# A transformer block on one core: rows gathered by computed numbers, two expert blocks written out, gate scores turned around

## The chip, the cores and the metric

The kernel runs on one core of one Trainium2 chip. The metric is the device time in microseconds (us) of one launch; lower is better. Of the kernel before there are three runs: 826.24, 819.68 and 824.00 us, median 824.0.

Engines: TensorE (PE) multiplies, VectorE (DVE) and ScalarE (ACT) work elementwise, GpSimd (POOL) does small work and issues DMAs on a queue of its own, SyncE (SP) only issues DMAs, on another queue.

## The reference, cut to what matters

```python
x = x + tanh(g_xattn) * xattn(ctx, layernorm(x))     # 4 x 512 rows of 512
x = x + tanh(g_ffn)   * ffn(layernorm(x))

# xattn: sim = Q K^T per batch (512 x 512), its top 30% of each row kept,
#        A = sigmoid(sim) * mask;  (1-gamma) * input + gamma * (A + A^T) / 2
# ffn:
scores = xt @ gate_w.T                               # 2048 tokens, 8 experts
p, e = top_k(softmax(scores), 2);  p = p / p.sum()
y_e = (silu(xt @ w1[e].T) * (xt @ w3[e].T)) @ w2[e].T   # 512 -> 1024 -> 512, f32
out = sum over the two chosen experts of p_e * y_e
```

Counted with the reference on its own inputs, the experts get 504, 573, 522, 490, 526, 482, 490 and 509 tokens (expert 0: 240 of them from the first 1024 tokens).

## The kernel before

The work has two parts. Part 1 computes the new x for 4 batches of 4 tiles (128 rows each), finds for each token its two experts, and sorts the tokens by expert. Part 2 runs the expert layers in blocks of 128 tokens.

**Part 1, for batch b.** ACT takes the sigmoid of the similarities, DVE masks them (`mask_A`, L993), PE adds A and its transpose (`add_transposed`, L502 and L504), ACT copies the sum out of PSUM (`even_rows`, L685), DVE adds it to x (`x1`, L1001), and SP stores the new x into `out`. ACT sums the squares (`spreads`, L697), POOL makes scale and shift of the second layernorm (`row_scales`), ACT writes the normalised rows (`normal_rows`, L705). PE computes the gate scores (`even_scores`, L513) with the rows as stationary operand and the gates (8 columns) moving. DVE chooses the two best experts (`choose`, L1028 to L1078), PE ranks the tokens within their expert (`ranks`), and POOL scatters each row, with the expert weights and the token's number behind it, into the expert's region of `routed` in DRAM (`route`, L399): per batch 4 tiles times 2 choices, 32 scatters in all. After the last batch, DVE writes `table`: first and last block of each expert.

**Part 2.** One loop over the experts holds a loop over the blocks of an expert; every engine runs the same two loops and they meet through semaphores. In a block g:
- PE runs the first layer in two halves of 512 columns (gate into one bank, up into another, each product as three fp32r matmuls: high times high, low times high, high times low; L546 to L548), transposes h of half 0 (L568), the rows of block g+1 (`transpose_x`, L553) and h of half 1, and runs the second layer into bank 7. The second layer's first piece waits for `hT_set[0]`, the low part of h's transpose.
- ACT makes silu (L754), the high parts of h's transposes (L758) and of the next rows (L750).
- DVE makes the product (L1128), the low parts (L1132 for h, L1116 for x), and scales y by the expert weight (L1140).
- POOL adds y into `out` with an indirect DMA that accumulates (`add_blocks`, L434): it waits for `y_set`, computes `y_row` (L432), drains (L433) and issues.
- SP loads the rows of the next block from `routed` as soon as `xtile` is free (L324).

The weights of an expert are 6 MB in three pieces (`raw`). POOL issues the loads of expert e+1's pieces at the head of its loop over e (L442), when the low parts of expert e's pieces have been made. In the last block of an expert, ACT and DVE also split the arrived weights into high (`w_hi`, L670) and low parts (`w_lo`, L1010). For expert 0 this happens ahead of the loop (`first_low`, L1022, and `split_high`).

The number of blocks is 35: the tokens of each expert divided by 128, rounded up. Each engine's instructions run in the order in which the code writes them; there is no scheduler.

## Time and profile before

| | |
|---|---|
| median of three runs | 824.0 us (819.68 to 826.24) |
| the profiled execution, its own time | 824.68 us |
| its span | 823.0 us |
| PE busy | 732.0 us, 89% |
| DVE busy | 396.6 us, 48% |
| ACT busy | 286.8 us, 35% |
| POOL busy | 146.9 us, 18% |
| mean granted clock of TensorE | 0.918 |

The span is the profiled execution from its first to its last instruction. Busy times are of instructions that compute or issue a DMA; the sequencers' own steps (waits, drains, register loads) are not counted. Matmuls overlap, so a busy PE need not be at its peak.

### The profile page before, as it was taken

To read this page: it belongs to the slowest core of one execution; us is meant where nothing else is said; L and a number is where in the kernel's file an instruction comes from. 1 tells how busy PE (TensorE), PEld (TensorE's weight loads), DVE (VectorE), ACT (ScalarE), POOL (GpSimd) and SP (SyncE) were. 2 spreads that over 40 slices of the span, in tenths; PEclk is the share of its full clock that TensorE was granted. 3 is DMA by queue.
4 is the path that set the end of the run, shared out by engine and by line. 5 is a ranking of instruction groups with operands and counts; after the bars stand their busy time and mean duration, and the time that the engine had idled before them with its cause. 6 is when DMAs were issued, how large, how long until landed. Compare 5 with 4: busy or idle time off the path is not lost.

```text
span 823.0 us, 10904 instructions
## 1 busy us (share of the span) xinstructions
PE 732.0 (89%) x3370; PEld 589.9 (72%) x3371; DVE 396.6 (48%) x930; ACT 286.8 (35%) x475; POOL 146.9 (18%) x199
## 2 busy tenths in 40 slices
PE   7393079556999999999999999999999999999996
PEld 3193046545888888888888888888888888888885
DVE  3988966562247232832266229222652382265222
ACT  4754647621135211711154116112531261253111
POOL 1371002782111000011001011010011110101110
PEclk9655577568999999999999999999999999999999
DMA  8842032655622721182115511821155127211111
GB/s 302 324 161 102 12 142 106 239 200 191 231 38 62 288 41 43 26 324 46 39 26 180 203 26 26 331 38 39 35 197 177 28 40 315 51 36 29 26 30 22
DMA packets 23727, 98.18 MB, mean 119 GB/s; under 512 B 2784, under 2 KB 3040, under 8 KB 19872
## 3 DMA queue, kind: packets, MB, share of 16 engines
q0 software_dynamic: 10992, 66.21, 26.0%
q1 hardware_dynamic: 12576, 31.81, 11.3%
q8 instruction: 4, 0.07, 0.0%
q14 instruction: 11, 0.09, 0.0%
q10 hardware_dynamic: 144, 0.00, 0.0%
HBM read 73.72 MB, written 24.30 MB: 119 GB/s over the span
## 4 chain that ended last, share of the span: by engine, by line
issue 72%; DVE 9%; POOL 6%; PE 5%; POOLq 3%; ACT 2%; DVEq 1%; DMA 1%; SPq 0%; ACTq 0%
POOL out L434 4%; POOL routed L399 2%; DVE front L852 2%; PE bank L504 2%; POOLq L255 1%; POOLq L433 1%; PE bank L466 1%; PE bank L502 1%; DVE top L950 1%; DVE ln_stats L810 1%; DVE front L947 1%; DVE rows_own L827 1%; POOL raw L442 1%; ACT front L705 1%; PE bank L456 1%
## 5 line engine op out<-in xcount | busy, mean ns | idle before, releaser
L546 PE MATMUL bank<-w_hi,xT_hi 128*128 128x512 f32 x560 | 225.5, 403 | 3.3 <-DVE xT_lo L1116 3.3
L547 PE MATMUL bank<-w_hi,xT_lo 128*128 128x512 f32 x560 | 222.3, 397 | 0.0
L548 PE MATMUL bank<-w_lo,xT_hi 128*128 128x512 f32 x560 | 221.7, 396 | 0.0
L754 ACT ACTIVATE act_g<-bank 128x512 f32<-128x512 f32 x70 | 41.8, 596 | 332.1 <-PE bank L548 327.6
L546 PEld LDWEIGHTS bank<-w_hi,xT_hi 128*128 128x128 f32 x560 | 105.8, 189 | 27.5 <-issue 3.7
L548 PEld LDWEIGHTS bank<-w_lo,xT_hi 128*128 128x128 f32 x560 | 105.6, 188 | 25.8
L547 PEld LDWEIGHTS bank<-w_hi,xT_lo 128*128 128x128 f32 x560 | 105.8, 189 | 23.5
L546 PE MATMUL bank<-w_hi,hT_hi 128*128 128x512 f32 x280 | 115.9, 414 | 0.0
L1132 DVE TENSOR_TENSOR hT_lo<-bank,hT_hi 128x512 fp32r<-128x512 f32 x70 | 48.4, 692 | 138.7 <-ACT hT_hi L758 138.7
L1010 DVE TENSOR_TENSOR w_lo<-raw,w_hi 128x1024 fp32r<-128x1024 f32 x88 | 104.3, 1221 | 19.0 <-ACT w_hi L670 10.5
L670 ACT ACTIVATE w_hi<-raw 128x1024 fp32r<-128x1024 f32 x88 | 91.4, 1061 | 59.3 <-PE bank L548 50.4
L548 PE MATMUL bank<-w_lo,hT_hi 128*128 128x512 f32 x280 | 110.0, 393 | 0.0
L547 PE MATMUL bank<-w_hi,hT_lo 128*128 128x512 f32 x280 | 109.9, 392 | 0.0
L1128 DVE TENSOR_TENSOR h<-bank,act_g 128x512 f32<-128x512 f32 x70 | 48.4, 691 | 96.9 <-PE bank L548 92.4
L432 POOL TENSOR_TENSOR y_row<-token_out,no_shift 128x1 int32<-128x1 int32 x35 | 6.4, 183 | 458.1 <-DVE token_out L1141 458.1
L1140 DVE TENSOR_SCALAR y<-bank,meta_now 128x512 f32<-128x512 f32 x35 | 26.3, 750 | 104.9 <-PE bank L548 99.4
L434 POOL DMA_INDIRECT out<-y,y_row x35 | 58.1, 1661 | 86.2 <-issue 86.2
L548 PEld LDWEIGHTS bank<-w_lo,hT_hi 128*128 128x128 f32 x280 | 52.8, 189 | 11.5
L547 PEld LDWEIGHTS bank<-w_hi,hT_lo 128*128 128x128 f32 x280 | 53.1, 190 | 8.7
L546 PEld LDWEIGHTS bank<-w_hi,hT_hi 128*128 128x128 f32 x280 | 53.2, 190 | 8.5
L758 ACT ACTIVATE hT_hi<-bank 128x512 fp32r<-128x512 f32 x70 | 41.7, 595 | 20.6 <-PE bank L568 19.8
L568 PE MATMUL bank<-ident,h 128*128 128x128 f32 x280 | 42.4, 275 | 1.5 <-issue 1.5
(190 smaller groups left out, 668.8 us busy)
## 6 DMA issues: line engine op xcount, KB each, us to landing
raw<-weights POOLq DMA_DIRECT2D x21, 2048.0 KB, 15.7
xtile<-routed SPq DMA_DIRECT2D x36, 260.5 KB
raw<-weights SPq DMA_DIRECT2D x3, 2048.0 KB, 7.9
xb<-x SPq DMA_DIRECT2D x4, 1024.0 KB, 11.3
raw<-xT SPq DMA_DIRECT2D x4, 1024.0 KB, 9.0
w_hi<-weights POOLq DMA_DIRECT2D x2, 2048.0 KB, 10.3
out<-xb SPq DMA_DIRECT2D x4, 1024.0 KB, 4.2
routed<-pad SPq DMA_DIRECT2D x8, 260.5 KB, 2.3
```

Source lines behind the costliest of these rows:

```text
L434: nc.gpsimd.indirect_dma_start(out, bass.IndirectOffsetOnAxis(ap=y_row[:, 0:1], axis=0), y[:, :], None, bounds_check=TOKENS + P - 1, oob_i ...
L546: nc.tensor.matmul(out_ap, hi, hi_w, start=start, stop=False)
L547: nc.tensor.matmul(out_ap, lo, hi_w, start=False, stop=False)
L548: return nc.tensor.matmul(out_ap, hi, lo_w, start=False, stop=stop)
L568: last = nc.tensor.transpose(bank[H_BANK[s]][:, c * P:(c + 1) * P], h[:, s, c * P:(c + 1) * P], ident[:, :])
L670: nc.scalar.activation(w_hi[q][:, j, :], raw[:, q, j * OPW:(j + 1) * OPW], ACT.Copy).then_inc(hi_set[q], 1)
L754: nc.scalar.activation(act_g[:, s, :], bank[GATE[s]][:, :], ACT.Silu).then_inc(silu_set[s], 1)
L758: nc.scalar.activation(hT_hi[:, s, :], bank[H_BANK[s]][:, :], ACT.Copy).then_inc(hhi_set[s], 1)
L1010: V.tensor_tensor(w_lo[q][:, j, :], raw[:, q, j * OPW:(j + 1) * OPW], w_hi[q][:, j, :].bitcast(F32), ALU.subtract).then_inc(lo_set[q], 1)
L1128: V.tensor_tensor(h[:, s, :], bank[UP[s]][:, :], act_g[:, s, :], ALU.mult).then_inc(h_set[s], 1)
L1132: V.tensor_tensor(hT_lo[:, s, :], bank[H_BANK[s]][:, :], hT_hi[:, s, :].bitcast(F32), ALU.subtract).then_inc(hT_set[s], 1)
L1140: V.tensor_scalar(y[:, :], bank[Y_BANK][:, :], meta_now[:, bass.ds(e, 1)], None, ALU.mult).then_inc(y_out, 1)
```

## The change

1. **No rows are scattered.** x1 is stored twice, into `out` and into `found` (one row per token in its own order, 128 rows of padding ahead). Behind each row stand its expert weights, its number, and scale and shift of its layernorm (`meta`, stored for two batches at a time; `store_meta`). `normal_rows` and `route` are gone.
2. **Blocks gather their rows.** POOL's `gather` is an indirect DMA from `found` into `xtile` by 128 row numbers in `rows_now`. ACT normalises the gathered rows in place (`normal_x`), one pass of 128x512 per block. SP has no part in the loop any more.
3. **Row numbers are computed.** For each of the 32 picks DVE writes a one-hot matrix of the slot (128x128), and DVE or POOL two of the column (128x136 each, times the partition's or the tile's number); PE multiplies them into `rows_ps` (`all_blocks`, 32 matmuls of 272 columns), DVE sorts the columns by block with table entries read one by one (`order_blocks`). For the two first blocks of expert 0, which take their tokens from the first half and from what follows, a smaller version is used (`early_slots`, `early_blocks`, `early_rows`).
4. **Two blocks are written out** ahead of the loops on all engines, with the choice for the second half of the tokens, the table and the row numbers between their instructions. The choice runs for two batches at a time.
5. **Scores.** `even_scores` has the gates as stationary operand (8 columns) and the rows moving (512 columns); ACT copies the 8x512 result, PE turns it back with four transposes per batch (`turn_scores`).

```diff
@@ sync @@
-            sp.wait_ge(early_set, 1)
-            early_full = sp.value_load(early_blocks[0:1, 0:1], min_val=0, max_val=TOKENS // P)
...
-                        sp.dma_start(xtile[:, :], routed[bass.ds(e * REGION + j * P, P), :]).then_inc(xtile_in, 16)
...
+                sp.dma_start(found_x[b], xb[:, b, :, :]).then_inc(x1_found[b], 16)
                 sp.dma_start(out_tiles[b], xb[:, b, :, :]).then_inc(x1_stored[b], 16)
@@ gpsimd @@
-            row_scales(0)
-            row_scales(1)
-            route(0, range(TB))
...
+            def gather(at):
+                nc.gpsimd.indirect_dma_start(
+                    xtile[:, :], None, found, bass.IndirectOffsetOnAxis(ap=at, axis=0),
+                    bounds_check=P + TOKENS - 1, oob_is_err=True,
+                ).then_inc(xtile_in, 16)
...
+            def add_y(g, and_next_x=True):
...
+                pool.wait_ge(y_set, g + 1)
+                nc.gpsimd.tensor_tensor(y_row[:, :], token_out[:, :], no_shift[:, :], ALU.add)
+                pool.drain()
+                if and_next_x:
+                    gather(rows_now[:, 0:1])
+                nc.gpsimd.indirect_dma_start(
+                    out, bass.IndirectOffsetOnAxis(ap=y_row[:, 0:1], axis=0), y[:, :], None,
...
+            pool.wait_ge(xtile_free, 1)
+            gather(rows_now[:, 0:1])
+            columns_of_first(range(PICKS // 4, PICKS))
+            add_y(0, and_next_x=False)
+            next_weights(0)
+            pool.wait_ge(xtile_free, 2)
+            gather(rows_now[:, 0:1])
+            add_y(1)
+            pool.wait_ge(table_set, 1)
+            add_blocks(0)
+            with pool.Fori(1, E - 1) as e:
+                next_weights(e)
                 add_blocks(e)
@@ tensor @@
+                for c in range(DC):
+                    last = nc.tensor.matmul(turned_ps[b], gate_c[:, c, :], even[b][:, c, :], start=(c == 0), stop=(c == DC - 1))
...
+            for g in range(WRITTEN):
...
+                if g == 1:
+                    all_blocks(0)
+                    all_blocks(1)
+                pe.wait_ge(hT_set[0], nth)
...
+                pe.wait_ge(hT_set[1], nth)
+                for k in range(1, OPS):
...
+                    if k == OPS - 1:
+                        transpose_x(nth + 1)
+                    second_layer([2 * k, 2 * k + 1]).then_inc(piece_done[2], 1)
@@ scalar @@
+            def normal_x(n):
...
+                act.wait_ge(xtile_in, n * 16)
+                nc.scalar.activation(xtile[:, 0:D], xtile[:, 0:D], ACT.Identity, bias=xtile[:, SHIFT:SHIFT + 1],
+                                     scale=xtile[:, SCALE:SCALE + 1]).then_inc(xn_set, 1)
...
                         silu(0, nth)
+                        normal_x(nth + 1)
                         silu(1, nth)
@@ vector @@
+            slots(1)
+            x_low(2, rows=False)
+            columns_of_second()
+            scale_y(0, 0, OPS)
+            take_meta()
...
+            tabulate()
+            product(0, 2, 2 * OPS)
+            h_low(0, 2)
+            product(1, 2, 2 * OPS)
+            order_blocks()
+            next_rows(2).then_inc(xtile_free, 1)
+            h_low(1, 2)
+            x_low(3)
```

How the order moves is shown at three places. The first is POOL's queue at the head of part 2, in the kernel before: weights (L442), then per block y_row and the adding scatter (drains and waits don't show as rows).

```order
L399 DMA routed<-rows_own,place_i 17408x521 x8
L439 UNCONDITIONAL_BRANCH
L439 ISA
L442 ISA
L442 DMA raw<-weights 128x4096
L442 ISA
L442 DMA raw<-weights 128x4096
L442 ISA
L442 DMA raw<-weights 128x4096
L255 REGISTER_ALU
```

And the same place of the change: scatter of block 0, weights of expert 1 (L471), the gather for block 2 (L426), then block 1 and a block of the loop.

```order
L459 TENSOR_TENSOR y_row<-token_out,no_shift 128x1
L463 DMA out<-y,y_row 2176x512
L471 DMA raw<-weights 128x4096 x3
L426 DMA xtile<-found,rows_now 128x523
L459 TENSOR_TENSOR y_row<-token_out,no_shift 128x1
L426 DMA xtile<-found,rows_now 128x523
L463 DMA out<-y,y_row 2176x512
L286 TENSOR_LOAD table
```

The loads of x's rows, which stood on SP's queue, now stand on POOL's, between y_row and the scatter, and behind the weights where these come first.

The second place is a block without new weights on ACT, before:

```order
L753 REGISTER_ALU
L754 ACTIVATE act_g<-bank 128x512 x2
L758 ACTIVATE hT_hi<-bank 128x512
L749 REGISTER_ALU
L750 ACTIVATE xT_hi<-bank 128x512
L758 ACTIVATE hT_hi<-bank 128x512
```

and now (L884 is silu, L834 is `normal_x`, L888 the high part of h, L839 that of x):

```order
L884 ACTIVATE act_g<-bank 128x512
L833 ISA
L834 ACTIVATE xtile<-xtile 128x512
L884 ACTIVATE act_g<-bank 128x512
L888 ACTIVATE hT_hi<-bank 128x512
L839 ACTIVATE xT_hi<-bank 128x512
L888 ACTIVATE hT_hi<-bank 128x512
```

`normal_x`, which waits for the gather, stands ahead of silu of half 1 and of both high parts of h.

The third is DVE in block 1 of the change, where nothing stood before but product and low parts: the end of `order_blocks` (one of its eight table loads is shown), the row numbers of block 2, then `h_low(1)` (L1353), for which PE's second layer waits.

```order
L286 TENSOR_LOAD table
L286 ISA x2
L1324 ISA
L1324 TENSOR_SCALAR rows_at<-scratch,part_no 128x17
L1328 TENSOR_SCALAR rows_now<-zero,rows_at 128x1
L1353 TENSOR_TENSOR hT_lo<-bank,hT_hi 128x512
L1333 COPY meta_next<-xtile 128x8
```

DVE's low part of h now stands behind the whole of `order_blocks`.

## Rows read from the trace of the kernel before

**Rows 1.** The page's slices: granted clock of TensorE, in tenths, 40 equal slices.

```profile
PEclk9655577568999999999999999999999999999999
```

**Rows 2.** Timeline, PE: start, us, engine, line, op, out<-in, count, [idle before <-releaser].

```profile
174.64 0.79 PE L546 MATMUL bank<-w_hi,xT_hi 128*128 128x512 f32 x1 [3.34 <-DVE xT_lo L1116]
...
194.87 1.11 PE L553 MATMUL bank<-ident,xtile 128*128 128x128 f32 x4 [4.76 <-DMA xtile<-routed]
...
196.21 0.63 PE L547 MATMUL bank<-w_hi,hT_lo 128*128 128x512 f32 x1
...
203.30 0.40 PE L546 MATMUL bank<-w_hi,xT_hi 128*128 128x512 f32 x1
...
797.30 0.40 PE L546 MATMUL bank<-w_hi,xT_hi 128*128 128x512 f32 x1
```

**Rows 3.** Timeline, POOL, around the weights of expert 2.

```profile
260.49 1.97 POOL L434 DMA_INDIRECT out<-y,y_row  x1 [0.92 <-issue]
261.91 2.26 POOL L442 DMA_DIRECT2D raw<-weights  x3
276.59 0.18 POOL L432 TENSOR_TENSOR y_row<-token_out,no_shift 128x1 int32<-128x1 int32 x1 [12.42 <-DVE token_out L1141]
284.54 1.67 POOL L434 DMA_INDIRECT out<-y,y_row  x1 [7.76 <-issue]
```

**Rows 4.** Lines L433 and L442: count, durations in ns min/median/max; time to landing.

```profile
L433 POOLq DRAIN  x35: 357/360/12912, 204.5 to 816.5; - x35
...
DMA to landing us min/median/max: 7.8/15.7/20.7
```

**Rows 5.** Timeline, POOL: two of the 32 scatters of rows.

```profile
170.36 1.97 POOL L399 DMA_INDIRECT routed<-front,place_i  x1 [0.30 <-issue]
...
176.18 0.98 POOL L399 DMA_INDIRECT routed<-front,place_i  x1 [0.30 <-issue]
```

**Rows 6.** The chain that ended last (start, us, what), and landing times of L434.

```profile
188.78 2.81 DMA routed<-rows_own,place_i
...
DMA to landing us min/median/max: 4.6/4.9/5.3
```

**Rows 7.** Timeline of DVE, groups by form (busy, mean ns | idle), and line L255.

```profile
125.97 2.74 DVE L993 SCALAR_TENSOR_TENSOR front<-front,thr 128x512 f32<-128x512 f32 x4 [0.72 <-ACT front L676]
...
159.79 0.37 DVE L1031 MAX8 best<-score 128x8 f32<-128x8 f32 x4
...
164.96 0.17 DVE L1078 CAST place_i<-place_f 128x8 int32<-128x8 f32 x1
...
165.72 8.04 DVE L1022 TENSOR_TENSOR w_lo<-raw,w_hi 128x1024 fp32r<-128x1024 f32 x7
...
L852 DVE TENSOR_SCALAR_CACHE_REDUCE front<-front,probe 128x512 bf16<-128x512 f32 x24 | 16.6, 742 | 0.7
...
L705 ACT ACTIVATE rows_own<-xb,ln_o,ln_r 128x512 f32<-128x512 f32 x8 | 5.8, 801 | 0.0
...
L255 DVEq TENSOR_LOAD <-table x24: 300/303/321, 184.6 to 748.2; - x24
```

**Rows 8.** Timeline of the block that starts at 275.3.

```profile
280.41 0.60 ACT L754 ACTIVATE act_g<-bank 128x512 f32<-128x512 f32 x1 [9.10 <-PE bank L548]
...
286.42 0.69 DVE L1132 TENSOR_TENSOR hT_lo<-bank,hT_hi 128x512 fp32r<-128x512 f32 x1 [4.59 <-ACT hT_hi L758]
...
286.94 0.60 PE L553 MATMUL bank<-ident,xtile 128*128 128x128 f32 x4
287.29 0.48 PE L546 MATMUL bank<-w_hi,hT_hi 128*128 128x512 f32 x1
```

**Rows 9.** Timeline, POOL, the last scatter.

```profile
817.70 1.55 POOL L434 DMA_INDIRECT out<-y,y_row  x1 [0.92 <-issue]
```

**Rows 10.** The chain that ended last: PE in part 1.

```profile
119.53 0.86 PE bank L504 x2
...
121.69 4.33 PE bank L513 x32
```

More of the change, by code:

```diff
@@ L492, in _, with add_transposed @@
             nc.tensor.matmul(settled_ps, ones_f[:, :], settled[:, :], start=True, stop=True).then_inc(settled_mm, 1)
[L494 removed]
+            def add_transposed(b, tiles):
                 At = A[b % 2]
                 pe.wait_ge(A_set, b + 1)
[L498 removed]
+                for i in tiles:
                     if b > 0:
@@ new lines, in order_blocks @@
+            def order_blocks():
+                dve.wait_ge(rows_mm, 2)
+                V.tensor_copy(region_rows_at[:, :], rows_ps[:, 1, :])
+                dve.drain()
+                V.scalar_tensor_tensor(region_rows_at[:, :], region_rows_at[:, :], float(P), rows_ps[:, 0, :], ALU.mult, ALU.add)
+                dve.drain()
+                dve.wait_ge(table_set, 1)
+                for e in range(E):
+                    at = 0 if e == 0 else entry(dve, 0, e, 1, MOST_BLOCKS - 1)
+                    V.tensor_scalar(rows_at[:, bass.ds(at, PER)], region_rows_at[:, e * PER:(e + 1) * PER], part_no[:, :], None, ALU.max)
+                    dve.drain()
```

674 lines of the change are left out of this document (425 added, 249 removed).

## The prediction

> **What bounds it now.** I read the slices first. In the last thirty of forty TensorE (PE) has its full clock, 2.4 GHz; in the ten before that the granted clock lies between that and 1.2 GHz, since PE is starved there [rows 1]. Then the timeline of PE: the first block of the expert layers starts at 174.64, the second at 203.30, the thirty-fifth at 797.30 [rows 2]. So 33 blocks take 594.0 us, 18.0 each; only the first is long, 28.7: PE waits 4.76 us for the second block's rows, and behind that wait a matmul lasts 0.63 us, as at 1.2 GHz, not 0.40 [rows 2]. The kernel is a front, then a loop at the pace of PE. A change can gain only by starting block 2 (counted from 0; at 221.3 now) earlier, and it loses whatever it puts into the loop, once per block or once per expert.
>
> The third view is POOL's queue. A 2 MB piece of weights is issued there three times per expert. Each time, the next block's scatter waits: y_row is computed at 276.59, but the scatter comes at 284.54, with 7.76 us of idle before it [rows 3], where the last one of the kernel has 0.92 [rows 9]. Seven of the 35 scatters are like this, one per set of weights. The drain between y_row and the scatter is what lasts: median 0.36 us, up to 12.9; the three pieces land one after the other, 7.8, 15.7 and 20.7 us after issue [rows 4]. 284.54 is 22.6 us behind 261.91 [rows 3], so POOL goes on when the 6 MB have landed. Now that costs nothing: nobody needs the scatter within a block, and the next rows come over SP's queue.
>
> **The change, part by part.** *The loop.* x's rows now come by a gather on POOL, behind that drain. Everywhere else it is early enough: issued 2.4 us into a block (as the scatter at 817.70, behind a block that ends at 815.3 [rows 9]), wanted behind silu(0), at 5.7 (280.41 and 0.60 [rows 8]). But in the second block of experts 1 to 6 it meets the weights. I lay it into the block that starts at 275.3. The scatter stood at 284.54; in the last block of the expert before, a gather goes ahead of scatter and weights, and one indirect DMA takes 1.3 us of POOL (0.98 and 0.3 idle) [rows 5], so the weights and all behind them are 1.3 later: gather at 285.8. The trace has no gather. Nearest rows: a scatter's rows land in 2.81 us, a scatter-add in 4.9 [rows 6]. A gather adds nothing up, so I take 2.8: 288.6. Then ACT, in its order, has normal_x (0.80, as L705 [rows 7]), silu (0.60), h_high (0.6), and DVE h_low (0.69): 289.4, 290.0, 290.6, 291.3, and with 0.1 us from engine to engine PE can start its second layer at 291.6. It starts at 287.29 now, right behind the transposes of x at 286.94 [rows 8]. **The loss is 4.3 us**, six times: 26 us. Bounds: 2.2 if the gather lands in 2.0 and the weights aren't moved; 6.4 if it lands like a scatter-add. normal_x itself is hidden elsewhere, since ACT has nothing else between silu(0) and silu(1); in a block with new weights it delays one copy of w_hi by 0.75 us, and the copies behind it wait for PE anyway. If that cover were gone, it would cost 0.75 in each of seven blocks. No block is added: the reference's own choice on its inputs gives expert 0 504 tokens, 240 of them in the first half, so four blocks as before, and 35 in all.
>
> The Trainium skill has a rule on POOL's DMAs beside wide work of DVE (SBUF — State Buffer, "SBUF: two separate sides"): descriptors are written through a port that DVE can lock, and a DMA of 620 ns then takes 3100. The trace agrees in kind, not in size: the two rows of rival 3 below show one us. At the page's factor of five the sum would be some 30 us higher, by the rows' one us it is the 6 of that rival.
>
> *The front.* Choosing and placing now happen twice, for eight tiles at a time; block 0 starts after the first half. DVE's order decides. Its third masking starts at 125.97 and takes 2.74 [rows 7]; ACT now squares batch 0's rows (four passes of 128x512) later, so I let it end at 127.3. Behind it on DVE, up to the y of block 0: twelve subtracts of 1.15 (8.04 for seven [rows 7]), 13.8; two choices (one of four tiles runs from its MAX8 at 159.79 to 164.96 [rows 7], 5.4 with its ends; four more tiles and ten more small steps make it 9.2), 18.4; fifteen passes of 128x512 (x1, x_low, product, h_low, scale_y) at 0.69 [rows 8], 10.4; small steps, 2.1: 44.7. DVE waits too: PE has its first eight tiles at 121.7, where the gate scores start now, and then needs two times four 0.86 for the new scores, two more tiles and eight short transposes [rows 10], to 132.4, when DVE has been ready since 129.7; with 2.0 for the transposes of the second x, 4.7. New are 88 instructions of 128x128 or 128x136 that write one-hot rows: 128x8 takes 0.09, 128x512 0.74 [rows 7]. A line through both gives 0.24; a bf16 source may be quicker, down to 0.09. I take 0.16: 14.1 (8 to 21). The gate scores themselves took 4.33 us a batch [rows 10] and take four times 0.86 and four transposes, about 4: under 1 us of PE a batch, beside DVE. So y_set comes at 127.3 + 44.7 + 4.7 + 14.1 = 190.8, and behind it y_row, drain, scatter, then the weights of expert 1: 2.7 later, **193.5**.
>
> Block 0 itself starts near 160, 14 us earlier, and that gain isn't kept: block 1 needs the rows of block 2, whose gather stands behind these weights, with or without a drain, since pieces on this queue land in order [rows 4]. 193.5 + 20 (19 to 22, between a piece's 20.7 to landing and the 22.6 to the next indirect DMA, less its start) + 2 for the gather is 215.5; normal_x 0.8; PE has idled by then, so transposes at the slow level, 1.1 as at 194.87, and six matmuls at half the loop's pace (18.0 us for 72 and some transposes), 2.6 [rows 2]: block 2 starts at **220.0** instead of 221.3, a gain of 1.3. Also in block 1, DVE's eight loads of table entries (0.30 each plus arithmetic [rows 7]) stand ahead of h_low(1): some 7 us that PE would wait, covered by the longer wait for the gather. Without that wait they would be next.
>
> *The end.* The last gather stands ahead of the last scatter: the scatter stands at 817.70 now [rows 9]; 1.3 us more.
>
> **Sum.** 823.0 − 1.3 + 6 x 4.3 + 1.3 = 848.8 of span. The profiled execution took 824.68 for its 823.0, and that is 0.7 above the median of three: 848.8 + 1.7 − 0.7 = 850.
>
> **Rivals.**
> 1. *The clock falls too.* In the held block PE is idle for 2.7 us and again for 1.5. After 4.76 us of idle a matmul took 0.63 instead of 0.40 [rows 2], some ten times, 2 us lost. If that happens in the six blocks: 850 + 12 = 862. Against it: both idle pieces are much shorter than that one, with work between.
> 2. *The hold is nearly hidden.* The gather lands in 2 us and the weights aren't later: 2.2 per expert, 850 − 13 = 837.
> 3. *DVE delays POOL's DMAs.* Indirect DMAs took 1.97 us while DVE ran wide subtracts and 0.97 otherwise [rows 5]. DVE runs such subtracts when an expert's last gather, scatter and weights are issued. One us more for each of the gather and weights: six times 1, 856. This is the mechanism of the Trainium skill's rule above (SBUF — State Buffer).
> 4. *The gather isn't held* (the other side): the drain passes, or the gather's rows overtake the weights. From 0 us of hold on, only the front decides: block 1 then waits for the eight loads, block 2 starts near 217, and the end is 823.0 − 4 + 1.3 + 1 = 821, no change; if the one-hot instructions cost 0.09, 6 us less, 815, faster. Against it: all seven drains behind weights were long, none was short.
>
> **Chances.** Forecast (846 to 854) 0.55; the clock 0.14; nearly hidden 0.10; DVE's delay 0.05; not held 0.12; 0.04 for a front that is later than any of these. The range takes the forecast, the clock and the nearly hidden case: front 7 us better with 2.2 per expert gives 830; front 8 us worse with 6.4 gives 870, which need not meet: 829 to 868. A median can tell about 1% (8 us) from no change. Over 1% slower is above 832: all but rival 4 and a little of 2, 0.82. Within 1%: 0.13. Faster by over 1%: rival 4 with cheap one-hot work, 0.05.
>
> **What would show it.** PE should wait for normal_x or the gather in one block of each of experts 1 to 6, about 4 us, and in no other; the drain should last about 7 us there; silu(1) should follow normal_x late in these blocks. The first matmul of block 0 should stand near 160 and that of block 2 near 220. I am wrong if the loop has no waits (rival 4), if the waits are there at other places too, or if block 2 starts before 212.

## The result and the profile after

| | before | after |
|---|---|---|
| median | 824.1 us (819.68 to 826.24, 4 runs) | 867.9 us (863.37 to 869.25, 4 runs) |
| the profiled execution, its own time | 824.68 us | 868.96 us |
| its span | 823.0 us | 867.4 us |
| PE busy | 732.0 us | 749.6 us |
| POOL busy | 146.9 us | 186.2 us |
| mean granted clock of TensorE | 0.918 | 0.913 |

The changed kernel is slower: ratio 1.055, 95% interval 1.051 to 1.059. The forecast was 850 with a range of 829 to 868; the measured median lies on its upper edge, 18 us above the forecast.

The granted clock by slices, from the page of the kernel after. It answers to [rows 1]: where the kernel before has nines without a break, there are now six eights. Four of them are slices with a held block of the loop; the first is the end of block 1 and the last is the end of the kernel. The two held blocks with the shortest slow stretches don't show at this width.

```profile
PEclk9655599796899899998999999989999999899998
```

The front, from the timeline of PE (start, us, engine, line, op, out<-in, count, [idle before <-releaser]); it answers to [rows 2].

```profile
156.42 0.79 PE L608 MATMUL bank<-w_hi,xT_hi 128*128 128x512 f32 x1 [5.14 <-DVE xT_lo L1337]
...
181.81 0.50 PE L608 MATMUL bank<-w_hi,xT_hi 128*128 128x512 f32 x1 [0.15 <-DVE xT_lo L1337]
...
201.15 1.12 PE L630 MATMUL bank<-ident,h 128*128 128x128 f32 x4 [9.30 <-DVE h L1349]
...
218.74 0.79 PE L608 MATMUL bank<-w_hi,hT_hi 128*128 128x512 f32 x1 [7.24 <-DVE hT_lo L1353]
...
226.40 0.49 PE L608 MATMUL bank<-w_hi,xT_hi 128*128 128x512 f32 x1 [0.37 <-DVE xT_lo L1337]
```

Block 0 starts at 156.42 and block 1 at 181.81, 18 and 21 us earlier than before. In block 1 PE stands twice, for h (9.30) and for the low part of h (7.24), and block 2 starts at 226.40, which is 5.1 later than before. The timelines of DVE and POOL say what stands ahead of these waits:

```profile
176.84 3.05 DVE L1222 TENSOR_SCALAR xb<-from_one,slot 128x128 bf16<-128x128 bf16 x16
...
196.25 0.06 DVE L1235 MEMSET small<- 128x1 f32 x1 [7.21 <-POOL scratch L420]
...
217.56 0.23 DVE L1324 TENSOR_SCALAR rows_at<-scratch,part_no 128x17 f32 x1 [0.77 <-issue]
```
```profile
189.33 0.81 POOL L419 TENSOR_SCALAR scratch<-columns,column,part_no 128x136 bf16<-128x136 bf16 x1
...
199.64 2.29 POOL L471 DMA_DIRECT2D raw<-weights  x3
218.90 1.13 POOL L426 DMA_INDIRECT xtile<-found,rows_now  x1 [16.96 <-DVE rows_now L1328]
```

POOL writes its 24 one-hot columns of the second half from 173.5 to 195.8: 0.81 to 1.06 us each, but one of 2.46 beside DVE's wide subtracts, 0.93 on average. DVE, whose 16 one-hot slots take 3.05, is done with its own columns at 189 and stands 7.21 us for them, ahead of block 0's y. So the weights are issued at 199.64. In block 1 the eight parts of the table come one per 1.01 us up to 217.56. Expert 0's needs no table entry, so there are seven loads and not eight; between two parts DVE is idle for 0.77 to 0.81 us, of which 0.30 is the load and the rest is register work. Only then comes block 2's gather.

The loop, at the same place as [rows 3] and [rows 8]: the block behind the weights of expert 2. First POOL and ACT, then PE, then stretches of PE (us, busy and count of PE, PEld, DVE, ACT, POOL, granted clock, DMA share, GB/s).

```profile
268.51 2.23 POOL L471 DMA_DIRECT2D raw<-weights  x3
281.72 0.18 POOL L459 TENSOR_TENSOR y_row<-token_out,no_shift 128x1 int32<-128x1 int32 x1 [10.98 <-DVE token_out L1359]
290.83 1.11 POOL L426 DMA_INDIRECT xtile<-found,rows_now  x1 [8.93 <-issue]
...
294.32 0.81 ACT L834 ACTIVATE xtile<-xtile 128x512 f32<-128x512 f32 x1 [8.19 <-DMA xtile<-found,rows_now]
```
```profile
291.80 0.39 PE L610 MATMUL bank<-w_lo,xT_hi 128*128 128x512 f32 x1
295.19 0.66 PE L615 MATMUL bank<-ident,xtile 128*128 128x128 f32 x4 [3.00 <-ACT xtile L834]
296.88 0.80 PE L608 MATMUL bank<-w_hi,hT_hi 128*128 128x512 f32 x1 [1.04 <-DVE hT_lo L1353]
297.48 0.63 PE L609 MATMUL bank<-w_hi,hT_lo 128*128 128x512 f32 x1
...
302.59 0.40 PE L610 MATMUL bank<-w_lo,hT_hi 128*128 128x512 f32 x1
```
```profile
281.00:291.00 10.00, 10.00 (x47) 8.11 (x46) 1.57 (x5) 0.60 (x1) 0.36 (x2) 1.00 0.67 285
...
297.00:302.00 5.00, 5.00 (x14) 4.04 (x15) 1.97 (x6) 0.60 (x1) 0.00 (x0) 0.50 0.00 0
303.00:308.00 5.00, 5.00 (x23) 4.06 (x23) 1.07 (x4) 0.00 (x0) 0.18 (x1) 1.00 0.00 0
```

The gather is issued 9.1 us behind y_row, where 1.2 us is usual, and its rows land 3.5 us behind that. PE idles 3.00 and 1.04 us, and after that it runs at a granted clock of 0.50 (the level of 1.2 GHz) up to 302.6: 14 matmuls in 5 us instead of 23. This block takes 25.1 us where an ordinary one takes 18.0. It is the longest of the six: they are 5.4 to 7.2 us too long. The waits of PE from 230 us on (waited for: us in total, times, longest) show that this happens in six blocks and nowhere else; below them the drain ahead of the gather (count, ns min/median/max), and the gather's time to landing.

```profile
PE bank L615 <- ACT xtile L834: 16.8, 6, 3.1
PE bank L608 <- DVE hT_lo L1353: 4.8, 6, 1.0
```
```profile
L460 POOLq DRAIN  x35: 448/451/8379, 197.2 to 859.3; - x35
```
```profile
DMA to landing us min/median/max: 3.4/3.5/4.3
```

Added up: block 2 starts 5.1 us later; from there to the end of the last block (858.0) it takes 631.6 us instead of 594.0, so 37.6 more for six held blocks, 6.3 each; from there to the end of the span 9.4 instead of 7.7, 1.7 more. 823.0 + 5.1 + 37.6 + 1.7 = 867.4, the span after.

### The profile page after: what moved, and what is told of

Read it like the earlier page. It is cut to its first block, busy times and chain, and to the rows that moved or that the text cites. A ratio compares the mean times of both kernels' runs of the same rounds, so it can differ in the third digit from the quotient of the medians.

```text
span 867.4 us, 10544 instructions
## 1 busy us (share of the span) xinstructions
PE 749.6 (86%) x3344; PEld 587.1 (68%) x3345; DVE 416.7 (48%) x1046; ACT 304.7 (35%) x497; POOL 186.2 (21%) x246
## 4 chain that ended last, share of the span: by engine, by line
issue 66%; DVE 11%; POOL 10%; PE 6%; POOLq 3%; DVEq 2%; DMA 1%; SPq 0%; ACT 0%
POOL out L463 5%; POOL xtile L426 2%; DVE front L988 2%; POOL scratch L420 1%; POOL scratch L419 1%; PE bank L554 1%; PE bank L516 1%; POOLq L460 1%; POOLq L286 1%; DVE top L1090 1%; PE bank L563 1%; DVE ln_stats L946 1%; DVE front L1087 1%; DVE scratch L963 1%; PE bank L552 1%
## 5 line engine op out<-in xcount | busy, mean ns | idle before, releaser
L884 ACT ACTIVATE act_g<-bank 128x512 f32<-128x512 f32 x70 | 41.6, 594 | 279.3 <-PE bank L610 279.3
L608 PE MATMUL bank<-w_hi,hT_hi 128*128 128x512 f32 x280 | 122.0, 436 | 15.0 <-DVE hT_lo L1353 15.0
L1353 DVE TENSOR_TENSOR hT_lo<-bank,hT_hi 128x512 fp32r<-128x512 f32 x70 | 48.3, 691 | 159.8 <-ACT hT_hi L888 159.8
L609 PE MATMUL bank<-w_hi,hT_lo 128*128 128x512 f32 x280 | 114.1, 407 | 0.0
L610 PE MATMUL bank<-w_lo,hT_hi 128*128 128x512 f32 x280 | 114.0, 407 | 0.0
L1150 DVE TENSOR_TENSOR w_lo<-raw,w_hi 128x1024 fp32r<-128x1024 f32 x88 | 104.1, 1225 | 14.8 <-ACT w_hi L797 13.7
L608 PEld LDWEIGHTS bank<-w_hi,hT_hi 128*128 128x128 f32 x280 | 55.8, 199 | 27.6 <-DVE hT_lo L1353 18.3
L426 POOL DMA_INDIRECT xtile<-found,rows_now x37 | 43.3, 1170 | 122.0 <-issue 81.0
L610 PEld LDWEIGHTS bank<-w_lo,hT_hi 128*128 128x128 f32 x280 | 55.5, 198 | 12.8
L609 PEld LDWEIGHTS bank<-w_hi,hT_lo 128*128 128x128 f32 x280 | 56.1, 200 | 9.2
L888 ACT ACTIVATE hT_hi<-bank 128x512 fp32r<-128x512 f32 x70 | 41.7, 595 | 50.6 <-PE bank L630 50.6
L463 POOL DMA_INDIRECT out<-y,y_row x35 | 55.8, 1593 | 11.5 <-issue 11.5
## 6 DMA issues: line engine op xcount, KB each, us to landing
raw<-weights POOLq DMA_DIRECT2D x21, 2048.0 KB, 15.7
```

What stands on the lines that cost most here:

```text
L426: nc.gpsimd.indirect_dma_start(xtile[:, :], None, found, bass.IndirectOffsetOnAxis(ap=at, axis=0), bounds_check=P + TOKENS - 1, oob_is_err ...
L463: nc.gpsimd.indirect_dma_start(out, bass.IndirectOffsetOnAxis(ap=y_row[:, 0:1], axis=0), y[:, :], None, bounds_check=TOKENS + P - 1, oob_i ...
L608: nc.tensor.matmul(out_ap, hi, hi_w, start=start, stop=False)
L609: nc.tensor.matmul(out_ap, lo, hi_w, start=False, stop=False)
L610: return nc.tensor.matmul(out_ap, hi, lo_w, start=False, stop=stop)
L884: nc.scalar.activation(act_g[:, s, :], bank[GATE[s]][:, :], ACT.Silu).then_inc(silu_set[s], 1)
```

## The experiments

Each kernel is the changed one with the edit shown, if nothing else is said. Times are medians; the kernel before took 820.7 to 824.6 beside them.

**1. Weights on the other queue.** The change's cost in the loop should vanish if POOL's queue is what holds the gather, and stay if it is the traffic.

```diff
@@ sync, at its end @@
+            with sp.Fori(0, E - 1) as e:
+                for q in range(GROUPS):
+                    sp.wait_ge(lo_set[q], OPS * e + OPS)
+                    sp.dma_start(raw[:, q, :], w_groups[bass.ds(e + 1, 1), q, :, :].squeeze(0)).then_inc(raw_in[q], 16)
@@ gpsimd @@
-            next_weights(0)
...
-                next_weights(e)
```

> The changed kernel with the loads of experts 1 to 7's weights issued by SP, each under the same wait for the low parts, and none of them on POOL. Theory (the gather is held on POOL because POOL's drain and queue stand behind the weights): no block of experts 1 to 6 waits for its rows, all 33 blocks from block 2 take 18.0 us, the span falls by the 37.6 us of the six held blocks, to about 830 us; block 2 still starts near 226, since its gather was issued at 218.9 by the row numbers' time. Rival (the gather is late because 6 MB of weights fill the DMA engines, whoever issues them): the waits stay, 850 to 868 us.

Measured: 830.4 us, ratio 1.009 (1.006 to 1.012). The waits of PE from 230 us on, all of them, and POOL in the block that was held:

```profile
PE bank L610 <- DVE hT_lo L1355: 1.0, 1, 1.0
```
```profile
279.45 0.18 POOL L463 TENSOR_TENSOR y_row<-token_out,no_shift 128x1 int32<-128x1 int32 x1 [12.70 <-DVE token_out L1361]
280.65 1.07 POOL L430 DMA_INDIRECT xtile<-found,rows_now  x1 [1.02 <-issue]
```

The gather comes 1.2 us behind y_row, as in any block. Block 2 starts at 224.17, 2.2 us earlier than in the changed kernel, which I had not expected. So of the 43.8 us that the change costs, 37.5 hang on the queue on which the weights are issued, those 2.2 included. One wait of 1.0 is left; what it is comes with experiment 7.

But the edit moves more than the queue. SP issues the three pieces between 251.4 and 265.2, where POOL issues them at 268.5, when its own loop gets there. The last piece lands at 274.0, and between 275 and 280 us no DMA moves anything (the last two numbers of the row, DMA share and GB/s):

```profile
275.00:280.00 5.00, 5.00 (x23) 4.12 (x22) 1.06 (x4) 0.00 (x0) 0.18 (x1) 1.00 0.00 0
```

So this run alone doesn't rule out its rival, that the traffic holds the gather whoever issues it. Experiments 7 to 9 do.

**2. The transposes of x later.** The loop has them ahead of the second piece of the second layer; here they stand ahead of its last piece, as in the two written-out blocks, with `normal_x`, `x_high` and `x_low` moved behind h.

```diff
@@ tensor, in the loop @@
-                    transpose_x(nth + 1)
                     pe.wait_ge(hT_set[0], nth)
...
+                    transpose_x(nth + 1)
                     pe.wait_ge(lo_set[2], split[3])
                     second_layer([6, 7])
```

> The changed kernel with the transposes of the next block's rows put ahead of the last two pieces of the second layer in the loop, as in the two written-out blocks, and normal_x and the high and low parts of x behind those of h; the weights stay on POOL. Theory (only the distance from the held gather's landing, 13.9 us into the block, to its use counts): use at about 16.4, no waits of PE, 830 us, perhaps 1 to 3 more where DVE's low part of x ends after 18.0 in blocks with new weights. Rival (PE is slowed by something else beside the weights, not by the wait for rows): 860 us or more.

Measured: 869.6, ratio 1.058 (1.053 to 1.062): none of what was expected. The late rows no longer hold anything, but every block is now 19.0 us long. From 230 us on the only wait of PE is the first row below; the second is its place in an ordinary block.

```profile
PE bank L608 <- DVE xT_lo L1338: 19.0, 32, 1.5
```
```profile
319.75 0.49 PE L608 MATMUL bank<-w_hi,xT_hi 128*128 128x512 f32 x1 [0.35 <-DVE xT_lo L1338]
```

Only six matmuls, 1.4 us, stand between the transposes and the first matmul of the next block, and two copies have to run in between. That gives 0.35 us of idle and a gap in the matmuls around it, 1.0 us in each block, and 1.45 of idle and 2.1 us in all in the blocks in which DVE and ACT also split weights. 33 blocks of one us and more pay for what six blocks save. My expectation had 1 to 3 us in all for this, and not what the early place is good for. The time alone would have spoken for the rival, 860 or more; the waits show that it is this cost and not the rival's.

**3. normal_x behind silu(1) and h_high(0)**, in blocks without new weights.

```diff
@@ scalar, blocks without new weights @@
                         silu(0, nth)
-                        normal_x(nth + 1)
                         silu(1, nth)
                         h_high(0, nth)
+                        normal_x(nth + 1)
                         x_high(nth + 1)
```

> The changed kernel with normal_x behind silu of half 1 and behind the high part of h of half 0, on ACT in blocks without new weights. PE still waits 3.0 us for the transposes of x in the six held blocks, but no longer 1.0 for the low part of h. If the loss of 6.3 a block is 4.0 of waits and 2.2 of slower matmuls, and the clock falls all the same: 6 times 1.0 less, 862 us. If the clock fell because of the second wait: 6 times 3.2 less, 849 us. Rival (the order on ACT doesn't matter): 868 us.

Measured: 855.9, ratio 1.041 (1.037 to 1.046). The held block, in PE's timeline and in stretches:

```profile
294.56 1.12 PE L615 MATMUL bank<-ident,xtile 128*128 128x128 f32 x4 [2.86 <-ACT xtile L834]
```
```profile
295.00:297.00 2.00, 2.00 (x9) 1.60 (x8) 0.66 (x4) 0.60 (x1) 0.00 (x0) 0.50 0.43 77
298.00:303.00 5.00, 5.00 (x24) 4.12 (x23) 0.82 (x2) 0.45 (x1) 0.00 (x0) 1.00 0.00 0
```

PE still waits 2.86 us for the rows, but not a second time, since silu(1) and h's high part are ready; and the clock is back at 1.00 by 298, where in the changed kernel it stays at 0.50 up to 302.6. This is again the longest of the six. In the four last of them PE waits 1.8 to 2.4 us and the clock doesn't fall at all, as in the third:

```profile
483.00:487.00 4.00, 3.06 (x18) 2.62 (x19) 1.55 (x5) 2.01 (x3) 0.00 (x0) 1.00 0.51 66
```

So the order in ACT's queue decides over the second wait and over most of the slow stretches: 12 us in all, although an ordinary block has become 0.27 longer (18.24). The time lies between my 862 and 849. Both had taken the first wait as unchanged, but it is shorter too (13.7 us in six blocks instead of 16.8), so how much of the clock's part is due to which wait is not separated.

**4. Only the row numbers that are needed first.** Expert 0's part of the table is put in place ahead of block 2's gather, the other seven behind `h_low(1)`.

```diff
@@ vector @@
-                for e in range(E):
-                    at = 0 if e == 0 else entry(dve, 0, e, 1, MOST_BLOCKS - 1)
-                    V.tensor_scalar(rows_at[:, bass.ds(at, PER)], region_rows_at[:, e * PER:(e + 1) * PER], part_no[:, :], None, ALU.max)
+                V.tensor_scalar(rows_at[:, 0:PER], region_rows_at[:, 0:PER], part_no[:, :], None, ALU.max)
...
             h_low(1, 2)
+            order_rest()
```

> The changed kernel with only expert 0's row numbers computed ahead of block 2's gather and of h_low of block 1, and the seven experts with a table load each behind it. PE's wait of 7.2 us for the low part of h in block 1 should go. Theory of the prediction (this gather stands behind the weights issued at 199.6, landed at 220.3): block 2 starts at most 1 to 2 us earlier, 866 us. Rival (the gather isn't held there, having no drain ahead of it, and only the row numbers were late): it lands near 215, block 2 starts 8 to 9 us earlier, 859 us.

Measured: 864.4, ratio 1.052 (1.047 to 1.057). POOL and ACT:

```profile
198.95 2.29 POOL L471 DMA_DIRECT2D raw<-weights  x3
210.35 1.12 POOL L426 DMA_INDIRECT xtile<-found,rows_now  x1 [9.12 <-DVE rows_now L1332]
...
220.36 0.81 ACT L834 ACTIVATE xtile<-xtile 128x512 f32<-128x512 f32 x1 [10.38 <-DMA xtile<-found,rows_now]
```

The gather is issued 8.5 us earlier and its rows are there only 10 us later, 21.4 us behind the weights' issue. There is no drain ahead of this gather. So the weights hold a gather in two ways: a drain lets it be issued only when they have landed, and one that is issued without a drain has its rows only 0.6 us behind the last piece (landed at 219.7). Block 2 starts at 224.70. The Trainium skill says in "DMA: Bandwidth & Descriptors" (Two DMAs through the same engine are not ordered) that within one queue of one DMA engine descriptors start in order. These rows agree with it.

**5. POOL's columns shared out.** Six of POOL's picks of the second half (12 of 24 instructions) go to DVE.

```diff
@@ gpsimd @@
-            columns_of_first(range(PICKS // 4, PICKS))
+            columns_of_first(range(PICKS // 4, PICKS - 6))
@@ vector, at the head of columns_of_second @@
+                for m in range(PICKS - 6, PICKS):
+                    i, k = m // 2, m % 2
+                    V.tensor_scalar(in_column[0][:, m, 0, :], columns[:, :], column[:, 0, i, k:k + 1], part_no[:, :], ALU.is_equal, ALU.mult)
+                    V.tensor_scalar(in_column[0][:, m, 1, :], columns[:, :], column[:, 0, i, k:k + 1], tile_no[:, i:i + 1],
+                                    ALU.is_equal, ALU.mult)
```

> The change, with 6 of POOL's second-batch picks (12 of its 24 column instructions of 128x136) given to DVE. Theory (the front is late because POOL's column instructions take 0.81 to 0.98 us each, which the prediction didn't price, and DVE stands 7.2 us for them ahead of block 0's y): POOL ends some 11 us earlier, DVE has 12 x 0.2 = 2.4 us more to do, so y_set(0), T of the weights and all behind them come 4.8 us earlier; the wait for the gather of block 2 moves by the same, block 2 starts near 221.6 instead of 226.4, and the time is 867.9 - 4.8 = 863. Rival (DVE itself is what is late, by one-hot instructions of 0.19 to 0.23 instead of 0.16, and the wait for POOL only covers it): DVE's work gets 2.4 us longer, no gain or a loss of up to 2.4: 868 to 870.

Measured: 863.4, ratio 1.049 (1.044 to 1.053). POOL and PE:

```profile
193.78 0.19 POOL L459 TENSOR_TENSOR y_row<-token_out,no_shift 128x1 int32<-128x1 int32 x1 [7.01 <-DVE token_out L1364]
```
```profile
197.71 1.11 PE L630 MATMUL bank<-ident,h 128*128 128x128 f32 x4 [4.86 <-DVE h L1354]
...
222.62 0.50 PE L608 MATMUL bank<-w_hi,xT_hi 128*128 128x512 f32 x1 [0.36 <-DVE xT_lo L1342]
```

As the theory had it. POOL now waits for DVE, not DVE for POOL, and block 2 starts 3.8 us earlier. An instruction of this shape takes 0.81 us or more on POOL; on DVE the next one starts 0.23 us later.

**6. The old scores.** The rows stationary, the gates moving, 16 matmuls of 8 columns per batch, no turning back.

```diff
@@ tensor, even_scores @@
-                for c in range(DC):
-                    last = nc.tensor.matmul(turned_ps[b], gate_c[:, c, :], even[b][:, c, :], start=(c == 0), stop=(c == DC - 1))
+                for i in range(TB):
+                    for c in range(DC):
+                        last = nc.tensor.matmul(scores_ps[b // 2][:, b % 2 * TB + i, :], even[b][:, c, i * P:(i + 1) * P], gate_c[:, c, :],
+                                                start=(c == 0), stop=(c == DC - 1))
```

> The change, with the gate scores as in the kernel before: rows as stationary operand, 16 matmuls of 8 columns for a batch, written where they are wanted, no copy and no turning back. Prediction's claim: the turned form saves under 1 us of PE a batch beside DVE, so this kernel is within 1 us of the changed one: 867 to 869. Rival 1 (the turned form shortens the path in the front): block 0 starts 3 to 6 us later, but what that costs is at most what reaches block 2's gather: up to 871. Rival 2 (the turned form with its copies and transposes lengthens the path to the choice): earlier by 1 to 2 us: 866.

Measured: 870.8 (863.5 to 874.1), ratio 1.060 (1.056 to 1.065). Block 0 starts at 161.97, 5.6 us later than in the changed kernel, y_row of block 0 comes 4.7 later and block 2 at 229.63, 3.2 later. That is rival 1: the turned scores do shorten the path to block 0, and a part of that reaches block 2. Whether it reaches the end can't be told: the time itself moved less than its runs are apart.

**7. Weights on SP, and fewer row numbers first**; and the same with POOL's columns shared out. The seven other parts of the table stand behind block 1's y here.

> The change with two edits: the weights of experts 1 to 7 are issued by SP instead of POOL, and of the eight parts of the table of row numbers only expert 0's is put in place ahead of block 2's gather and h_low(1); the other seven come behind block 1's y (right as long as expert 0 has at least four blocks, as it has here). Theory: row_first gained only some 2 us since its gather, issued 8.5 us earlier, then stood behind the weights in POOL's queue; with these on another queue the gather is issued near 209.7, lands 3.5 us later, and PE's transposes of the rows come at 214.2 instead of 221.2; block 2 starts near 216.3 instead of 224.2 (the kernel with the weights on SP alone): 830.4 - 7.9 = 822.5. Rival (the weights' own traffic holds the gather, whatever the queue, or the seven table loads now delay block 2): 828 to 831.

> The three edits together: weights on SP, only expert 0's row numbers ahead of block 2, and 12 of POOL's column instructions on DVE. Theory: the three costs stand one after the other on the path to block 2, so they add: 830.4 - 7.9 - 4.8 = 817.7, block 2 near 211.5, and the kernel is faster than the one before by 0.8%. Rival (behind POOL's columns DVE's own order is next, so the split gives at most 2 us here): 820 to 822, no difference from before that can be told.

Measured: 827.7 (825.2 to 834.8), ratio 1.007 (1.004 to 1.009), and 828.7 (824.7 to 832.9), ratio 1.005 (1.003 to 1.008). Both missed. Block 2 does start early, at 217.65 and 217.42. What took it back, from the second kernel (POOL, ACT, PE):

```profile
172.97 1.17 POOL L430 DMA_INDIRECT xtile<-found,rows_now  x1 [13.31 <-DMA found<-meta]
```
```profile
181.69 0.81 ACT L836 ACTIVATE xtile<-xtile 128x512 f32<-128x512 f32 x1 [6.37 <-DMA xtile<-found,rows_now]
```
```profile
230.33 1.12 PE L632 MATMUL bank<-ident,h 128*128 128x128 f32 x4 [2.86 <-DVE h L1360]
```

Three things. First, SP issues expert 1's weights at 168.7, and block 1's gather, issued into this traffic at 172.97, lands after 8.7 us instead of 3.5. DVE stands 4.55 us for these rows (for their high part, up to 184.41), so that the shared-out columns gain nothing: y_row comes at 196.25, not at 193.8. Second, the seven table parts make the product of block 2 late by 2.86 us, and the slow clock behind it takes more: from y_row to y_row this block takes 23.1 us, 18.7 with the weights on SP alone. Third, in single blocks of the loop a gather is issued into the traffic of the weights and lands late: in the second kernel the weights of one expert are issued from 430.0 to 444.2, the gather at 442.1, and ACT has its rows at 450.5, 8.4 us later. Each such block is 1.2 to 3.9 us longer. Three of them are the same blocks in both profiles, but by other amounts, and the second kernel has one more; this may be what spreads the runs. The one wait left in experiment 1 is of this kind (its gather took 7.7 us). So a gather beside the weights on another queue is not free of them. But it isn't held until they have landed, as on POOL's: the gather of 172.97 has its rows at 181.7, ahead of the second piece (183.5), and that of 442.1 ahead of the third (454.1). All three were mended in the next step.

**8. The gather as early as it can go.** Every block from block 1 on issues the next gather as soon as the tile is free, ahead of y_row, drain and scatter. The wait is carried by an addition of zeros into an added buffer `spare`, four bytes a partition.

```diff
@@ gpsimd, add_y @@
+                if and_next_x:
+                    pool.wait_ge(xtile_free, g + 2)
+                    nc.gpsimd.tensor_tensor(spare[:, :], no_shift[:, :], no_shift[:, :], ALU.add)
+                    gather(rows_now[:, 0:1])
                 pool.wait_ge(y_set, g + 1)
                 nc.gpsimd.tensor_tensor(y_row[:, :], token_out[:, :], no_shift[:, :], ALU.add)
                 pool.drain()
-                if and_next_x:
-                    gather(rows_now[:, 0:1])
```

> The change, weights still on POOL, but in every block from block 1 on POOL issues the next gather as soon as the tile is free (some 14 us into the block before) and ahead of y_row, its drain and the scatter. Theory (what holds the rows is the 6 MB ahead of them in POOL's queue, and a gather without a drain ahead waits there too): in the block behind the weights the gather is issued near 14 us into the block before, but its rows land only when the weights have, 20 to 23 us behind their issue, some 9.5 to 11 us into the held block, which is 3 to 4 us earlier than in the changed kernel, since neither drain nor issue nor its own 3.5 us come behind them: PE's waits shrink from 4.0 to 0 to 1 us and the clock stays up: 867.9 minus 6 x 5.3 to 6.3, 830 to 836, and the landing time of these six gathers is over 10 us. Rival 1 (only the drain held it): landing 3.5 us in all of them, no waits, 829. Rival 2 (the rows begin to move only when all of the weights have landed and need 3.5 us from there): waits of 2 to 3 us stay, 850 to 858.

> The same early gather, with the weights of experts 1 to 7 issued by SP. Theory (on another queue the weights cost the gather only contention: some gathers issued under their traffic landed after up to 9.1 us instead of 3.5, and that made one or two blocks late): with 14 us of lead no block waits for its rows, and the last gather no longer stands ahead of the last scatter: 830.4 - 1.3 (end) - 1.6 (the one late block) = 827.5. Rival (POOL's early issue with its wait in front delays y's scatter or the next rows): 830 or more.

> All repairs together: early gather; weights on SP, those of expert 1 only once block 1's rows have landed; 12 of POOL's column instructions on DVE; only expert 0's row numbers ahead of block 2, each other expert's at the head of the loop over the expert before it (one us each, right as long as each expert has two blocks or more and expert 0 four). Theory: y of block 0 near 193.8 as with the columns split, block 2 some 20.9 us behind it as with only one table part ahead (196.8 to 217.7 there), at 214.7; then 33 blocks of 18.0 and 8.1 to the end: 816.8 of span, 818. Rival (in three_parts the seven table parts behind block 1 cost a wait of 2.9 us and a slow stretch; if the single ones at each expert's head cost DVE the same, product of half 0 is late once per expert): 818 + 7 x 1 = 825, no gain on the kernel before.

Measured: 819.3 (ratio 0.997, 0.995 to 0.999), 820.5 (0.998, 0.995 to 1.000) and 807.3 (0.983, 0.980 to 0.986; one of its six runs took 1497 us, for which I have no explanation, the others 806.9 to 808.2). The last ratio's interval reaches across 0.98, so whether it is 2% faster is unclear; that it is faster is clear. None of the three has a wait of PE left from 230 us on. With the weights on SP, all 33 gathers of the loop land after 3.3 to 3.6 us, nine of them issued while weights are moving:

```profile
DMA to landing us min/median/max: 3.3/3.5/3.6
```

That rules out the rival of experiment 1, in which the traffic alone holds them. But each kernel is 7 to 11 us faster than its theory, and the blocks take 17.73 us, not 17.97. The next experiment takes this apart; its kernel without the added buffer is the one to read for the gather alone.

**9. The four bytes.** `spare` behind `y_row` moves all later buffers by 32 bytes a partition, since the program rounds their addresses up. Two kernels have it without any new instruction, two have the early gather or all repairs without it.

```diff
         y_row = sb("y_row", [P, 1], I32)
+        spare = sb("spare", [P, 1], I32)
```

> The changed kernel with an unused buffer of four bytes a partition behind y_row, as the kernels with the early gather have it; no instruction differs. Theory A (where the buffers lie sets the pace of the first layer's matmuls, 0.227 us apart instead of 0.233): blocks take 17.73 us where they aren't held, 33 x 0.24 = 8 us less, 860. Theory B (the gather's time in the block sets it): 868, matmuls 0.233 apart.

> The early gather with weights on POOL, its waiting instruction writing into an unused column of an existing buffer, so that no buffer moves. Theory A (where the buffers lie): blocks of 17.97 again, 819.3 + 8 = 827. Theory B (when the gather runs): 819.

> The kernel before with the same unused buffer behind y_row. Theory A: if its blocks of 18.00 us have the same cause, 33 x 0.24 = 8 us less at most, 816 (its y_row stands behind other small buffers, so it may also be unmoved: 824). Theory B: 820 to 824, no change.

> All repairs together as in best, without the added buffer. Theory A: 807.3 + 8 = 815. Theory B: 807.

Measured: the changed kernel with the buffer 863.0 (ratio 1.046, 1.041 to 1.051), blocks of 17.73 us; the early gather without it 829.0 (1.005, 1.004 to 1.007), blocks of 17.96; the kernel before with it 824.0 (1.001, 0.998 to 1.004), blocks of 18.03; all repairs without it 816.5 (0.992, 0.988 to 0.995). Theory A holds in the family of the changed kernel: some 8 us of the gain in experiment 8 have nothing to do with the gather. The spans of the profiled executions are 825.6 against 817.9 for the early gather and 813.8 against 805.3 for all repairs. The medians differ by 9.7 and 9.2, but they come from two chips, on which the kernel before took 820.7 and 824.6. A group of first-layer matmuls by shape (busy, mean ns) between 230 and 860 us, of the changed kernel and with the buffer:

```profile
L609 PE MATMUL bank<-w_hi,xT_lo 128*128 128x512 f32 x523 | 206.2, 394 | 0.0
```
```profile
L610 PE MATMUL bank<-w_hi,xT_lo 128*128 128x512 f32 x521 | 202.8, 389 | 0.0
```

And this is the early gather without it, POOL and ACT at the place that was held, and the time to landing:

```profile
265.51 2.23 POOL L473 DMA_DIRECT2D raw<-weights  x3
274.15 0.19 POOL L460 TENSOR_TENSOR rows_at<-no_shift 128x1 int32<-128x1 int32 x1 [6.41 <-DVE rows_now L1330]
274.90 1.10 POOL L426 DMA_INDIRECT xtile<-found,rows_now  x1 [0.56 <-issue]
```
```profile
287.39 0.82 ACT L836 ACTIVATE xtile<-xtile 128x512 f32<-128x512 f32 x1 [2.90 <-DMA xtile<-found,rows_now]
```
```profile
DMA to landing us min/median/max: 3.4/3.5/12.5
```

The gather is issued 9.4 us behind the weights, lands 21.9 us behind them, after 12.5 us instead of 3.5, and PE's transposes of these rows come 2.2 us after they are normalised. So the rows wait in the queue as they did in experiment 4, and nothing waits for them. It is so in all six places: the rows land after 9.9 to 12.5 us, 0.6 to 0.7 behind the last piece of the weights. That rules out that only the drain held them. The medians give 867.9 - 829.0 = 38.9. The profiled executions are 41.7 us apart: 39.2 from block 1's y_row to the last one, 1.4 behind it, where the last gather is out of the last scatter's way, and 1.1 in the front.

## Why the prediction was right or wrong, point by point

- **What is held, and where: right.** One block each of experts 1 to 6, no other; PE waits for `normal_x`; the cause is the weights ahead in POOL's queue. w_on_sp removes it, early_no_pad removes it in another way. Rival 4 is out: on POOL's queue no gather passed the weights, with a drain or without.
- **The size of the hold: wrong; this is the step that failed most.** The term was 6 x 4.3 = 26; it measured 37.6, 11.8 more. The delay itself was worked out well: I had the gather 10.5 us into the block, the rows 13.3 and the second layer 16.3; in the block shown (it starts at 280.43) they stand at 10.4, 13.9 and 16.45. The gather lands after 3.5 us, not 2.8, and the steps behind it are shorter by 0.4. Of the 6.3 us, 3.6 are idle time of PE (21.6 in six blocks) and the rest is slow clock. What failed is the step "rival 1: both idle pieces are much shorter than that one, with work between", which I used to give the slow clock only 0.14. Idle of 3.00 and 1.04 us with 0.66 of work between was enough for the level of 0.50. The price of that rival, 2 us a block more (6.3, 862), was right: 6.3 was measured. nx_behind shows how much hangs on the lengths: behind 2.86 us alone the clock is back within some 3 us, behind both waits it takes nearly 6, and behind 1.8 to 2.4 us alone it stayed up.
- **The front: the mechanism right, the term wrong by 6.4.** Block 0 came at 156.4 (near 160 predicted), and its gain was not kept, as predicted. Block 2 came at 226.4, not 220.0. The step that failed is y_set, which I worked out from DVE's list alone: POOL's 24 columns had no price in it. With 0.93 us each they end last, and DVE stands 7.2 us for them. cols_split gives 3.4 us of it back at the weights' issue. DVE's own new instructions were also above my 0.16, with 0.19 to 0.23, within the bounds. The table loads, seven and not eight, were priced (7 us, 7.24 measured) and placed rightly as what comes next: row_first took them away and gained 1.7 at block 2, since the weights stood there too.
- **The landing of the weights:** 7.8, 15.7 and 20.7 us are the shortest, median and longest of all 21 pieces, not one expert's three, as I wrote; those of expert 2 took 11.1, 15.9 and 20.4. That they land one after the other is right, and the 20 us that I used stands.
- **The scores:** "under 1 us of PE a batch, beside DVE" missed what counts. The old form starts block 0 5.6 us later. It hardly changes the sum, since that start is not kept.
- **normal_x at nothing in the other blocks, and the end:** the first holds (17.97 against 18.00 us a block); the end cost 1.7 where I had 1.3.
- **DVE's delay of POOL's DMAs (rival 3):** beside DVE's wide subtracts an issue of the gather took 1.37 us (265.75) and 1.09 otherwise, in the front up to 1.54. The Trainium skill ("SBUF — State Buffer", "SBUF: two separate sides") has a factor of five for a DMA beside a copy on DVE. DVE's work here is subtracts of two inputs, so it isn't the same case; in the changed kernel the factor is 1.4 at most, and in the loop it hides.
- **The sum:** the front 6.4, the holds 11.8, the end 0.4: 848.8 + 18.6 = 867.4. All three errors have the same sign. The range's upper corner, a late front together with the long hold, had been worked out as 870 and then cut to 868 with the remark that the two need not meet. They met.

What stays open: why 32 bytes change the pace of the first layer in the changed kernel and not in the kernel before. In both they move the operands of the first layer (`xT_hi`, `xT_lo`) from 32 bytes past a multiple of 64 to a multiple of 64, so that alone isn't the cause. Also open is why a gather beside weights on another queue took 3.3 us at one place and 9.1 at another.

## What to carry to other kernels

A load that a block needs soon must not be issued behind bulk loads on the same queue, whether there is a drain between or not: either put the bulk on another queue, or issue the small load so early that it may wait out the bulk. Price a wait of PE of three us together with the slow clock behind it, and look at what ACT has queued behind the instruction that waits, because that decides how long the slow stretch is. Where two engines share a job, price both lists; and before a gain of one per cent is put down to an edit, run the edit's buffers without its instructions.

## What the runs showed of the hardware that I had not expected

- A tensor_scalar of 128x136 bf16 takes 0.81 us on POOL while DVE stands and 0.91 beside DVE's one-hot instructions, once 2.46 beside its wide subtracts, and 0.23 from one to the next on DVE. The Trainium skill ("GPSIMD Engine Reference", Engine selection) calls POOL about two times slower than DVE for two inputs and says of one input that it is "roughly line-rate"; here, with one input, the ratio is 3.5.
- A gather of 128 rows lands after 3.5 us. Beside weights on another queue it took 3.3 to 9.1. Behind 6 MB on the same queue its rows were there 19.3 to 22.0 us after the issue of the weights and 0.6 to 0.7 behind their last piece, whenever it was issued itself (9.4 to 11.4 us behind them).
- A shift of the buffers by 32 bytes changed a block from 17.97 to 17.73 us in the changed kernel and did nothing in the kernel before. With all repairs it is worth some 8 us; in the changed kernel itself 5, since its held blocks got no shorter (24.4 to 25.3 us, 23.4 to 25.1 without it).
- All repairs together make the gathered rows pay: 816.5 without the shift and 807.3 with it, 0.8% and 1.7% faster than the kernel before, where the change as it was made is 5.5% slower.
